# Running the adjacency's split and transpose ahead of the scores in a two-layer graph network kernel

## The reference, cut to what matters

```python
q, k, v = x @ Wq.T + bq, x @ Wk.T + bk, x @ Wv.T + bv
a = q @ k.T / sqrt(512) + adj + adj
x1 = layernorm(x + softmax(a) @ v)
h = relu(adj @ (x1 @ W1) + b1)            # W1: 512 x 128
out = layernorm(x1 + adj @ (h @ W2) + b2)
```

## Time and profile before

| | |
|---|---|
| runs | 1905.51 us median of 3 (1905.25 to 1905.91) |
| profiled execution | 1905.41 us, span in the profile 1903.6 us |
| busy | PE 1896.3, DVE 1085.0, ACT 861.9, POOL 115.9 us |
| DMA | 463.73 MB, mean 244 GB/s |
| score stage | about 178 to 1537 us |
| first convolution, PE | 1539.8 to 1709.7 us |
| second convolution and output | to the end |

### The profile page before, as it was taken

One profiled execution on the slowest core, in us unless ns is written; L12 is line 12 of the kernel. 1 busy time (PEld: TensorE's weight loads), 2 busy tenths in 40 slices (PEclk: granted clock), 3 DMA queues, 4 the chain that ended last, 5 costly groups with the idle time before them and its releaser, 6 DMA issues.

```text
span 1903.6 us, 26546 instructions
## 1 busy us (share of the span) xinstructions
PE 1896.3 (100%) x9265; PEld 889.0 (47%) x9265; DVE 1085.0 (57%) x2107; ACT 861.9 (45%) x1848; POOL 115.9 (6%) x211
## 2 busy tenths in 40 slices
PE   9999999999999999999999999999999999999998
PEld 4444444444444444444444444444444454444446
DVE  7787666666666666666666666666666620001334
ACT  6655554555555555555555555455545611010112
POOL 0000000000000000000000000000000000002334
PEclk9999999999999999999999999999999999999999
DMA  8664599999999999999999999999999999989996
GB/s 253 164 140 113 134 232 230 225 231 225 223 225 227 225 230 232 222 229 220 230 228 226 228 226 226 229 223 225 228 218 240 215 354 387 387 301 360 394 394 243
DMA packets 801015, 463.73 MB, mean 244 GB/s; under 512 B 646768, under 2 KB 654704, under 8 KB 800880
## 3 DMA queue, kind: packets, MB, share of 16 engines
q1 hardware_dynamic: 792816, 448.03, 93.7%
q10 hardware_dynamic: 8064, 14.00, 2.0%
HBM read 220.99 MB, written 92.01 MB: 164 GB/s over the span
## 4 chain that ended last, share of the span: by engine, by line
PE 99%; DMA 0%; issue 0%; DVE 0%; ACT 0%; SPq 0%; POOL 0%; POOLq 0%; ACTq 0%
PE bank L597 15%; PE bank L599 15%; PE bank L598 15%; PE bank L719 12%; PE bank L721 12%; PE bank L720 12%; PE bank L842 5%; PE bank L844 5%; PE bank L843 5%; PE bank L625 1%; PE bank L806 0%; PE bank L802 0%; PE bank L803 0%; PE bank L863 0%; PE bank L865 0%; PE bank L864 0%
## 5 line engine op out<-in xcount | busy, mean ns | idle before, releaser
L1013 ACT ACTIVATE tsp<-ring,sc 128x512 f16<-128x512 f32 x248 | 179.0, 722 | 599.0 <-DMA tsp<-tsp 598.3
L1399 DVE SCALAR_TENSOR_TENSOR ring<-bank,sc,adj_in 128x512 f32<-128x512 f32 x256 | 192.2, 751 | 398.2 <-PE bank L599 392.9
L597 PE MATMUL bank<-xT,gT 128*128 128x512 f16 x1024 | 388.1, 379 | 0.0
L598 PE MATMUL bank<-xT,gT 128*128 128x512 f16 x1024 | 388.1, 379 | 0.0
L599 PE MATMUL bank<-xT,gT 128*128 128x512 f16 x1024 | 388.1, 379 | 0.0
L719 PE MATMUL bank<-xv,tsp 128*128 128x512 f16 x1008 | 382.0, 379 | 0.1
L720 PE MATMUL bank<-xv,tsp 128*128 128x512 f16 x1008 | 382.0, 379 | 0.0
L721 PE MATMUL bank<-xv,tsp 128*128 128x512 f16 x1008 | 382.0, 379 | 0.0
L1214 DVE SCALAR_TENSOR_TENSOR tsp<-adj_in,s_a,tsp 128x512 f16<-128x512 f32 x248 | 184.7, 745 | 46.3 <-ACT tsp L1021 45.8
L1214 DVE SCALAR_TENSOR_TENSOR tsp<-ring,sc,tsp 128x512 f16<-128x512 f32 x248 | 184.9, 746 | 0.1
L1001 ACT ACTIVATE ring<-ring,bias 128x512 f32<-128x512 f32 x256 | 181.0, 707 | 8.8 <-DVE bias L1416 8.8
(11 more groups left out here) (270 smaller groups left out, 2173.3 us busy)
## 6 DMA issues: line engine op xcount, KB each, us to landing
adj_in<-in_adj SPq DMA_DIRECT2D x256, 256.0 KB, 3.2
at_dram<-tsp SPq DMA_DIRECT2D x248, 256.0 KB, 3.2
xv<-at_dram SPq DMA_DIRECT2D x54, 1024.0 KB, 14.4
adj_in<-at_dram SPq DMA_DIRECT2D x29, 1024.0 KB, 14.4
xT<-at_dram SPq DMA_DIRECT2D x20, 1024.0 KB, 14.0
xv<-in_x SPq DMA_DIRECT2D x8, 1024.0 KB, 10.0
g_dram<-tsp SPq DMA_DIRECT2D x32, 256.0 KB, 4.0
gT<-g_dram SPq DMA_DIRECT2D x32, 256.0 KB, 3.6
```

The source lines that it names most:

```text
L597: pe.matmul(dst, ah, bh, start=first, stop=False)
L598: pe.matmul(dst, ah, bl, start=False, stop=False)
L1013: act.activation(p_split(e)[:, 0:BANK], p, ACT.Copy, scale=col[f"p_up{batch(TW * kb)}"]).then_inc(a_p, 1)
L1399: dve.scalar_tensor_tensor(t, s_bank[s % S_BANKS][:, :], col[f"k_l{batch(s // KB)}{batch(TW * (s % KB))}"], adj_in[:, s % AR, :], ALU.mult ...
```

## The change

The adjacency's path gets a step counter `v` of its own. `adj_plan` gives each step `s` a list of steps `v`: two at `s` = 0, 2 and 3, none at 9, two at 40, 72, 104, 136 and 168, one otherwise. So `v` is `s + 3` after step 3, `s + 2` from step 9, and `s + 7` from step 168 on. Loads, absolute sums, scales, halves, transposes and stores of the adjacency all go by `v`, on all engines.

Blocks 248 to 254 then pass through the common path within the 257 steps of the loop, and block 255 just behind it. PE's `adj_transposes` and the two `last_adj_` functions go, and so do their eight groups of PE transposes. `load_first_unit` now loads all four quarters (1 MB), and waits for the store of the last row block's part. In SP's list behind the loop the transpose and store of block 255 stand among the softmax transposes; the first unit is issued behind softmax block 252 instead of 251; units 8 and 9 are issued before 6 and 7. On ACT and DVE a few small steps of that list move.

```diff
-ADJ_AT = (1, 2, 4, 5, 7, 8, 10, 11)
+ADJ_STEPS = {0: 2, 2: 2, 3: 2, 9: 0, **{row * KB: 2 for row in range(5, 25, 4)}}
+ADJ_LEFT = 1
+def adj_plan():
+    plan, first = [], 0
+    for s in range(NS + 2 * KB):
+        count = ADJ_STEPS.get(s, 1)
+        plan.append(list(range(first, first + count)))
+        first += count
+    assert plan[NS][-1] == NS - 1 - ADJ_LEFT + ADJ_LAG
+    return plan
...
@@ SP, load_first_unit
-                last = TAIL - KB + kb
+                last = TAIL + kb
                 sp.wait_ge(d_ast[last % 2], 16 * (last // 2 + 1))
-                sp.dma_start(slots[kb][:, 0:TW - 1, :, :].rearrange("p r b n -> p r (b n)"), units_dram[LAST, kb][:, 0:TW - 1, :]
-                             ).then_inc(d_unit[kb], 16)
+                sp.dma_start(slots[kb].rearrange("p r b n -> p r (b n)"), units_dram[LAST, kb]).then_inc(d_unit[kb], 16)
...
@@ SP, in the loop over s
-                a = s - ADJ_LAG
-                if 0 < a <= NS:
-                    store_at(a - 1)
-                if 0 <= a < TAIL:
-                    transpose_adj(a)
+                for v in adj_steps[s]:
+                    a, q = v - ADJ_LAG, v + AHEAD
+                    if 0 < a <= NS:
+                        store_at(a - 1)
+                    if 0 <= a < NS:
+                        transpose_adj(a)
+                    if 12 <= q < NS:
...
+                        load_adj(q)
...
@@ SP, behind the loop
-            for i in range(KB):
-                if i:
-                    transpose_p(TAIL + i)
-                if i == 1:
-                    store_at(TAIL - 1)
-                if i == 3:
-                    load_first_unit(0)
-                if i == 5:
-                    store_x1(NT - 2)
-            load_first_unit(1)
-            load_first_unit(2)
+            transpose_p(TAIL + 1)
+            store_at(NS - 2)
+            transpose_adj(NS - 1)
+            for i in range(2, 5):
+                transpose_p(TAIL + i)
+            store_at(NS - 1)
+            load_first_unit(0)
+            transpose_p(TAIL + 5)
+            store_x1(NT - 2)
+            for i in range(6, KB):
+                transpose_p(TAIL + i)
+            for kb in range(1, 4):
+                load_first_unit(kb)
             sp.wait_ge(p_x1, 1)
             sp.wait_ge(d_x1, 16 * (NT - 1))
             sp.dma_start(xr[:, :], x[P * (NT - 1):P * NT, :]).then_inc(d_xr, 16)
-            for kb in range(3, KB):
+            for kb in range(4, 6):
                 load_first_unit(kb)
             for l in range(KB, KB + 2):
                 load_unit(l)
+            for kb in range(6, KB):
+                load_first_unit(kb)
...
@@ PE
-                if s - NS in ADJ_AT:
-                    adj_transposes(ADJ_AT.index(s - NS))
...
-                    if n == 0:
-                        pe.wait_ge(v_al, TAIL + kb + 1)
```

More of the change, by code:

```diff
@@ L318, in gnn_program @@
         end_bank = [bank[1], bank[4], bank[5]]
-        at_bank = bank[2:4]
         ht_bank = bank[4:6]
@@ L340, in gnn_program @@
         d_out = [sem(f"d_out{i}") for i in range(O_RING)]
-        p_xt, p_pre, p_v, p_g, p_qk, p_pv, p_y, p_adj, p_x1, p_unit, p_h, p_o, p_end = (
-            sem("p_" + s) for s in "xt pre v g qk pv y adj x1 unit h o end".split())
+        p_xt, p_pre, p_v, p_g, p_qk, p_pv, p_y, p_x1, p_unit, p_h, p_o, p_end = (
+            sem("p_" + s) for s in "xt pre v g qk pv y x1 unit h o end".split())
         a_rs, a_ws = sem("a_rs"), sem("a_ws")
@@ L355, in gnn_program @@
         loads, holds = unit_plan()
+        adj_steps = adj_plan()
         block = ctx.enter_context(nc.Block())
@@ L474, in load_first_unit @@
                     for i in range(2):
-                        sp.wait_ge(d_ast[i], 16 * TAIL // 2)
-                last = TAIL - KB + kb
+                        sp.wait_ge(d_ast[i], 16 * NS // 2)
+                last = TAIL + kb
                 sp.wait_ge(d_ast[last % 2], 16 * (last // 2 + 1))
-                sp.dma_start(slots[kb][:, 0:TW - 1, :, :].rearrange("p r b n -> p r (b n)"), units_dram[LAST, kb][:, 0:TW - 1, :]
-                             ).then_inc(d_unit[kb], 16)
+                sp.dma_start(slots[kb].rearrange("p r b n -> p r (b n)"), units_dram[LAST, kb]).then_inc(d_unit[kb], 16)
             def load_unit(l):
@@ L485, in load_unit @@
                 elif slot < KB + 3:
-                    sp.wait_ge(p_adj, min(3 + 4 * (slot - KB), KB))
-                    sp.wait_ge(v_al, TAIL)
+                    sp.wait_ge(v_add, NS)
+                    sp.wait_ge(v_al, NS)
                     if slot == KB + 2:
@@ L527, in _ @@
                         load_adj(q)
[L528 to L535, removed]
+                for v in adj_steps[s]:
[5 more added lines that the diff above has]
+                    if 12 <= q < NS:
+                        if q == AR - 1:
+                            sp.wait_ge(a_w1, 1)
+                            sp.wait_ge(v_w1, 1)
+                        if q >= AR:
+                            sp.wait_ge(v_al, q - AR + 1)
+                        load_adj(q)
                 if NS - Y_EARLY <= s + 1 < NS:
@@ L757, in h_transposes @@
                 last.then_inc(p_h, 1)
[L759 to L768, removed]
             for s in range(NS + LAG):
@@ L1021, in adj_hi @@
                 act.activation(asp[a % 2][:, 0:BANK], adj_in[:, a % AR, :], ACT.Copy, scale=s_a[:, r:r + 1]).then_inc(a_ah, 1)
[L1023 to L1030, removed]
             def x1_hi(r):
@@ L1064, in _ @@
                     exponentials(e)
[L1065 to L1069, removed]
+                for v in adj_steps[s]:
+                    if v + 1 < NS:
+                        absolute_sums(v + 1)
+                    if 0 <= v - ADJ_LAG < NS:
+                        adj_hi(v - ADJ_LAG)
                 if s >= 2 * KB and kb == X1_AT:
@@ L1075, in _ @@
                 exponentials(TAIL + i)
-                if i % 2:
-                    last_adj_hi(i // 2)
-                if i == 3:
+                if i < ADJ_LEFT:
+                    adj_hi(NS - ADJ_LEFT + i)
+                if i == 6:
                     y_hi(NT - 3)
[L1080 to L1083, removed]
+            last_x1_hi(NT - 2)
             y_hi(NT - 2)
@@ L1436, in adj_lo @@
                          ).then_inc(v_al, 1)
[L1438 to L1441, removed]
             def attention_rows(r):
@@ L1498, in _ @@
                         exp_bias(r)
[L1499 to L1504, removed]
+                for v in adj_steps[s]:
+                    if v % KB == KB - 1 and v < NS:
+                        adj_sum(v // KB)
+                    if v % KB == 0 and KB <= v <= NS:
+                        adj_scale(v // KB - 1)
+                    if 0 <= v - ADJ_LAG < NS:
+                        adj_lo(v - ADJ_LAG)
                 if s >= 2 * KB:
@@ L1516, in _ @@
                 p_lo(TAIL + i)
-                if i % 2:
-                    last_adj_lo(i // 2)
-                if i == 3:
+                if i < ADJ_LEFT:
+                    adj_lo(NS - ADJ_LEFT + i)
+                if i == 4:
                     attention_rows(NT - 2)
+                if i == 5:
+                    normalise(NT - 2)
+                if i == 6:
                     y_lo(NT - 3)
[L1522 to L1527, removed]
+            last_x1_lo(NT - 2)
             conv_scales()
@@ L1647, in _ @@
             pool.wait_ge(g_set, 3)
-            for s in range(KB - 1, NS + 2 * KB):
+            for s in range(NS + 2 * KB):
                 r, kb = divmod(s, KB)
-                if kb == KB - 1 and r < NT:
-                    pool.wait_ge(v_rs, r + 1)
-                    pool.partition_all_reduce(a_all[:, r:r + 1], a_row[:, r:r + 1], P, ALL_MAX).then_inc(g_asum, 1)
+                for v in adj_steps[s]:
+                    i = v // KB
+                    if v % KB == KB - 1 and i < NT:
+                        pool.wait_ge(v_rs, i + 1)
+                        pool.partition_all_reduce(a_all[:, i:i + 1], a_row[:, i:i + 1], P, ALL_MAX).then_inc(g_asum, 1)
                 if s >= 2 * KB and kb == STATS_AT:
```

## The result

The changed kernel takes 1916.69 us in the median (6 runs, 1914.6 to 1918.46), the kernel before 1905.72 (6 runs): ratio 1.0056, 95% interval 1.0044 to 1.0069. It is 11.0 us slower, where 4.4 were forecast and 1912.5 was the upper end of the range. The direction was right, the size was not.

What follows compares the result with a forecast made beforehand. PE bounds the kernel, with the DMA close behind. Last landing +4.7 +2.5 -0.3 = +6.9 us, less the 2.5 us lead, gives 1905.4 + 4.4 = 1909.8 us; PE's -3.8 vanishes in the wait. Range 1906 to 1912.5.

Steps and rivals of the forecast that it cites:

- PE transposes: Ahead of the first convolution: eight groups of PE transposes, 0.44 us each, go from the path, 3.5 us saved.
- The start: Ahead of the first `attend`: the first softmax transpose goes out earlier and PE's 0.3 us idle goes; doubled steps cost nothing.
- nothing idle at 222 us: Sign at the first `attend`: PE's idle place in the score stage is gone in the profile after.
- Doubled steps 40 to 168: Score stage: extra transposes, stores and loads fit in the DMA and SP's queue; 0 us, bounds 0 and 13.
- Rival 3: Score stage has no spare DMA capacity, so PE stalls up to 7 us; about 1915 us, chance 0.05.
- Softmax block 250: End of the score stage: PE stalls 1 to 1.5 us for its later transpose, not adding to the end.
- The loads: First eight units grow to 1 MB: seven quarters +4.7, later issue +2.5, start -0.3; last landing of convolution one +6.9 us.
- The first unit's issue: Sign at the end of the score stage: a move under 2 or over 5 us makes the forecast's size wrong.
- The last landing sets the end: Last unit of the first convolution: PE must wait for its load until 1711.5, ending the kernel 4.4 us later.
- the waits at units 6 and 7: Start of the first convolution: PE idles about 5 us together, as units 8 and 9 are loaded first.
- Rival 4: The wait at units 6 and 7 also lowers PE's clock, costing +2 us; 1911.8 us, chance 0.09.
- PE's busy time: Sign in the profile after: it falls by some 5 us, by the modelled durations of the transposes.

Runs made afterwards that it cites:

- e4: Kernel before, with only the changed kernel's doubled steps 0, 2, 3 and empty step 9, the lead given back by empty steps 40 and 48; 1910.30 us.
- e5: Changed kernel with its seven extra adjacency steps in row blocks 2, 6, ... 26, the first at step 16; 1911.75 us.
- e8: As e2, but ACT does the absolute sums of blocks 10 to 12 behind the first exponential, with explicit waits for the query stores; 1912.58 us.
- e12: Kernel before with seven doubled steps in row blocks 2 to 26, given back by seven empty steps between 216 and 240; 1905.60 us.
- e9: As e6, but the first unit's 1 MB load is issued behind the last softmax transpose instead of ahead of the last three; 1909.00 us.
- e15: As e9, but with units 8 and 9 loaded ahead of 6 and 7, as in the changed kernel; 1910.87 us.
- e2: Changed kernel with units 6 and 7 loaded ahead of 8 and 9, as before the change; 1914.95 us.
- e1: Changed kernel with its seven extra adjacency steps in row blocks 1, 5, ... 25, the first at step 8; 1915.04 us.
- e3: Changed kernel with the edits of e1 and e2 together; 1913.97 us.
- e6: As e5, but with units 6 and 7 loaded ahead of 8 and 9; 1912.10 us.

## Why the prediction was wrong

- **PE transposes, -3.5 us:** right. From the first `attend` to the first convolution PE took 1317.1 us before and 1320.9 in the changed kernel, in which 7.2 are lost: 1313.7, 3.5 less.
- **The start, -0.3 us: the step that failed, +5.0 in its place.** The prediction looked at SP, where step 9 loses its issues, and wrote of the doubled steps 0, 2 and 3 "two ACT sums and some issues where PE takes 5.2 us a step; nothing there". It counted their busy time and not their position: a lead of two steps also moves three sums, at steps 6 to 8, ahead of the first exponential, and two of them wait, 6.2 and 5.0 us, for loads that SP issued only at 204.9 and 213.1 us. Shown by e4 (+4.4 alone), e5 (-4.9 when undone) and e8 (order on ACT, 5.2 to 1.3). The prediction's own sign, nothing idle at 222 us, failed too. With this step undone the time is 1911.75, inside the range; this alone put the result outside.
- **Doubled steps 40 to 168, 0:** right (e12: 1905.60; the changed kernel lost nothing between 232 and 1500 us). Rival 3, no room in the DMA, fell.
- **Softmax block 250, 1 to 1.5 us:** there, a little smaller (0.7 in the changed kernel, 0.5 to 1.3 in the runs with all eight blocks moved). Not foreseen was the wait for block 253, 2.2 us with 1.7 of slow clock, with a bulk load in front of it.
- **The loads: right mechanism, and the size of the last landing was near.** Forecast +6.9; e9, with a clean start, had 1710.8 against 1704.6, +6.2, and e5 1712.1, +7.5. The first unit's issue moved from 1519.0 to 1527.9, 8.9 us, where more than 5 was to be a sign of a wrong size; in e5 it moved 4.7. Where the last landing did set the end (e9) the time is 3.3 us over the kernel before, for 4.4 forecast.
- **"The last landing sets the end": wrong for this order of units.** In the changed kernel and in e5 PE waits so long at unit 6, and so much more in the slow clock behind it, that 1.6 and 2.4 us of lead are left at the last unit. So e5's place inside the range is in part luck: it ends by another path than the forecast's. The prediction had the waits at units 6 and 7, "about 5 us together", 4.3 by the trace, but took them as part of the final sum. Rival 4 named what was missing, at +2: e15 against e9 gives 1.9, the changed kernel against e2 1.7, e1 against e3 1.1, but e5 against e6 -0.35. It had a chance of 0.09 and should have gone with the forecast, since the forecast itself put a wait of 5 us there. The rows show PE at 2.4 GHz before the wait and at 1.2 behind it; the rule of the Trainium skill ("TensorE: Matmul & The Clock Gate", "Part 1: The HAM clock gate"), by which an idle array falls back to 1.2 GHz, agrees. PE's busy time rose, from 1896.3 to 1898.0 us, where a fall of some 5 us was forecast: a slow matmul is shown as 0.63 us, not 0.38.
- Sum for the medians, one edit after the other: start 4.9 (changed kernel to e5), first unit behind the transposes 0.9 (to e15), order of units with the clock 1.9 (to e9), and 3.3 left over the kernel before, for bytes and the later place of the loads less the PE transposes. That makes 11.0 by construction. By the other way, over e6, the order is worth -0.35 and the first unit's place 3.1. So these two are not terms of their own; only their sum, 2.8, is the same either way. Left open: how often the long stop at block 253 occurs. By the profiles it did in the changed kernel, e6 and e8 and not in e1, e2, e3, e5, one execution each; why it takes the form of a near stop for 2 us was not tried.

## What to carry to other kernels

When a pipeline is moved ahead by n steps, list for each engine what, in its order, now stands in front of the first critical instruction and what each of these waits for; busy time says nothing of it. A PE saving of 0.44 us a block is no saving where the DMA, already a little slower than PE, pays 0.68 us for it. And a forecast that contains one wait of several us must also contain the slow matmuls behind it.

## What was unexpected of the hardware

- Behind waits of 2.2, 3.6 and 4.3 us in the changed kernel the granted clock fell to its lower level: 512-column matmuls started 0.43 us apart instead of 0.216, and 1.5 to 1.7 us more were lost each time. e5 waited 5.8 us at unit 6 and then lost 2.4. A wait of 2.6 us in e1, and those of 2.1 in e6 and e9, were followed by no such loss.
- A DMA transpose issued behind a 1 MB load landed in 8.4 us instead of 3.5, and while it stood there the transfers fell from 314 to 27 GB/s for about two us. In e1, e2, e3 and e5, without that long stop, it landed in 6.4 to 6.6 us; in the kernel before, behind 768 KB, the next transpose landed in 5.5.
- A stream of 1 MB loads from DRAM held 387 GB/s from 1570 to 1712 us in the changed kernel. The Trainium skill, "DMA: Bandwidth & Descriptors", "Where 436 GB/s comes from", gives about 358 as what binds one core there, as half of what a stack gives two cores; here only one core ran, and the measurement decides.
